# Moving a small transpose, a slot computation and a wait in a two-stage expert kernel, and a longer warm-up

## What is computed

```python
w = cond_weights[itok]                       # 32 x (32 x 32)
xc = einsum('bct,bcd->bdt', x, w)            # 32 x 32 x 256
xt = xc.reshape(T, 256)
probs = softmax(xt @ gate_w)
top_p, top_i = top_k(probs, 2)
for k in range(2):
    e, w = top_i[:, k], top_p[:, k]
    pos = position of the token among those of the same expert
    keep = pos < cap
    buf[e, pos] = xt                         # only where keep
    h = gelu(buf @ w1[e] + b1[e])
    y = h @ w2[e] + b2[e] + gelu(buf @ wd[e]) @ wu[e]
    out += y[e, pos] * keep * w
sh = gelu(xt @ sw1 + sb1) @ sw2 + sb2 + gelu(xt @ swd) @ swu
result = x + out + 0.2 * sh
```

## Time and profile before

| What | us |
|---|---|
| median of three runs | 211.71 |
| the three runs | 211.88, 208.94, 211.71 |
| the profiled execution | 210.92 |
| its span, from first to last instruction | 209.1 |
| outside the span | 1.82 |

### The profile page before, as it was taken

The page is one execution under the profiler, slowest core; times in us unless marked ns, Lnnn a source line. Parts: engine busy times, 40 slices in busy tenths (PEclk is TensorE's granted clock), DMA queues, the critical chain, the costliest instruction groups (busy, mean ns, idle before and its releaser), DMA issues.

```text
span 209.1 us, 3942 instructions
## 1 busy us (share of the span) xinstructions
PE 190.2 (91%) x1390; PEld 182.3 (87%) x1390; DVE 135.0 (65%) x294; ACT 133.9 (64%) x285; POOL 110.3 (53%) x162
## 2 busy tenths in 40 slices
PE   6669999999999499999999999999999999999900
PEld 6667777998789499999999999999999999999900
DVE  4547489744762105695879869869869968967020
ACT  2246799913890107968949949949949859778100
POOL 4401404078773006001794895885876867945662
PEclk9978999999999889999999999999999999999975
DMA  5599971522222895018867867866786787601423
GB/s 164 173 296 336 226 249 48 175 72 85 95 92 72 232 327 196 3 13 287 220 114 231 218 158 210 206 201 194 165 234 199 132 263 223 79 0 9 53 31 39
DMA packets 27897, 33.03 MB, mean 158 GB/s; under 512 B 4554, under 2 KB 24772, under 8 KB 27876
## 3 DMA queue, kind: packets, MB, share of 16 engines
q1 hardware_dynamic: 23748, 27.31, 42.7%
q0 software_dynamic: 3760, 4.89, 14.3%
q10 hardware_dynamic: 368, 0.56, 1.0%
HBM read 23.96 MB, written 8.79 MB: 157 GB/s over the span
## 4 chain that ended last, share of the span: by engine, by line
PE 73%; issue 6%; POOL 6%; DMA 6%; DVE 3%; POOLq 1%; ACT 1%; SPq 1%; DVEq 0%
PE hid_ps L791 10%; PE hid_ps L793 10%; PE hid_ps L792 10%; PE y_ps L791 9%; PE y_ps L793 9%; PE y_ps L792 9%; POOL slot_rows L418 5%; PE turn_ps L935 3%; DMA gate_raw<-in_L_ffn_gate_w 3%; DMA slot_rows<-token_row,slot_i 2%; PE row_ps L951 2%; DMA slot_in<-slot_rows 1%; PE hid_ps L812 1%; POOLq L51 1%; PE turn_ps L812 1%
## 5 line engine op out<-in xcount | busy, mean ns | idle before, releaser
L396 POOL DMA_INDIRECT out_rows<-y_row,slot_tok x24 | 44.8, 1866 | 15.8 <-DVE y_row L735 10.9
L618 DVE TENSOR_TENSOR hid_l<-gelu_f,hid_h 128x320 fp32r<-128x320 f32 (+1 forms) x80 | 41.8, 539 | 12.8 <-ACT hid_h L522 11.1
L791 PE MATMUL hid_ps<-xs_h,w_h 128*128 128x288 f32 x128 | 38.2, 298 | 0.0
L793 PE MATMUL hid_ps<-xs_h,w_l 128*128 128x288 f32 x128 | 37.6, 294 | 0.0
L793 PE MATMUL y_ps<-hid_h,w_l 128*128 128x288 f32 x128 | 37.6, 294 | 0.0
L792 PE MATMUL y_ps<-hid_l,w_h 128*128 128x288 f32 x128 | 37.6, 294 | 0.0
L791 PE MATMUL y_ps<-hid_h,w_h 128*128 128x288 f32 x128 | 37.6, 294 | 0.0
L792 PE MATMUL hid_ps<-xs_l,w_h 128*128 128x288 f32 x128 | 37.6, 294 | 0.0
L521 ACT ACTIVATE gelu_f<-hid_ps,bias_now 128x320 f32<-128x320 f32 x64 | 35.2, 549 | 0.9 <-PE hid_ps L793 0.4
L522 ACT ACTIVATE hid_h<-hid_ps,bias_now 128x320 fp32r<-128x320 f32 x64 | 35.5, 555 | 0.0
L594 DVE TENSOR_TENSOR w_l<-w_raw,w_h 128x512 fp32r<-128x512 f32 x36 | 26.4, 752 | 12.5 <-POOL w_h L364 11.8
(11 more groups left out here) (170 smaller groups left out, 413.9 us busy)
## 6 DMA issues: line engine op xcount, KB each, us to landing
w_raw<-in_L_ffn_w SPq DMA_DIRECT2D x16, 1024.0 KB
slot_rows<-empty_row SPq DMA_DIRECT2D x1, 2600.0 KB, 17.1
slot_in<-slot_rows SPq DMA_DIRECT2D x8, 260.0 KB, 3.7
x_in<-in_x SPq DMA_DIRECT2D x2, 512.0 KB, 4.6
w_raw<-in_L_ffn_sw SPq DMA_DIRECT2D x1, 1024.0 KB
out_rows<-base SPq DMA_DIRECT2D x2, 512.0 KB, 3.8
wu_raw<-in_L_ffn_wu SPq DMA_DIRECT2D x24, 32.0 KB
slot_in<-slot_rows SPq DMA_DIRECT2D x8, 65.0 KB, 3.7
```

Of the source, the lines that this page charges most:

```text
L396: pool.indirect_dma_start(out=out, out_offset=bass.IndirectOffsetOnAxis(ap=slot_tok[par][0:n, s:s + 1].bitcast(U32), axis=0), in_=y_row[0: ...
L618: dve.tensor_tensor(hid_l[:, j - 1, 0:n], gelu_f[:, j % 3, 0:n], hid_h[:, j - 1, 0:n].bitcast(F32), ALU.subtract).then_inc(hid_split, 1)
L791: pe.matmul(out_ap, l_h, r_h, start=start, stop=False)
L793: return pe.matmul(out_ap, l_l, r_h, start=False, stop=stop)
```

## The change

- On VectorE the transpose of the condition and the diagonal copies come ahead of the two chunks of `w1`, not behind them. VectorE makes three of the four copies and ScalarE one (`ACT_DIAG`).
- The warm-up has nine loops in place of five, so 144 matmuls in place of 80.
- `count_before` stands after hidden tile 4 of the first half in place of tile 6, and `place_tokens` after split 5 in place of after split 8.
- `turn_slots(0, 0)` stands after output tile 2 of the second half in place of tile 1, and VectorE's split of the slots after base row 6 in place of 5.

```diff
-WARM_UP = 5
+WARM_UP = 9
+ACT_DIAG = 1
...
-            for g in range(SPT // 2, SPT):
+            for g in range(SPT - ACT_DIAG, SPT):
                 rows = slice(g * C, (g + 1) * C)
                 act.activation(cond_diag[rows, :, rows], diag_v[:, g, :, :], ACT.Copy).then_inc(diag_act, 1)
...
-            for c in range(CHUNKS // 2):
-                w1_chunk(c, 0, 0)
             dve.wait_ge(cond_in, 16)
             dve.transpose(cond_t, cond_dc).then_inc(cond_turned, 1)
             dve.wait_ge(cond_turned, 1)
-            for g in range(SPT // 2):
+            for g in range(SPT - ACT_DIAG):
                 rows = slice(g * C, (g + 1) * C)
                 dve.tensor_copy(cond_diag[rows, :, rows], diag_v[:, g, :, :]).then_inc(diag_dve, 1)
+            for c in range(CHUNKS // 2):
+                w1_chunk(c, 0, 0)
...
                 if j == 2 or j == 3:
                     w2_chunk(CHUNKS // 2 + j - 2, 0, 0)
-            place_tokens()
+                if j == 5:
+                    place_tokens()
...
                 shared_row(t)
-                if t == HTILES + 1:
+                if t == HTILES + 2:
                     slots_lo_part(0)
...
-                pe.wait_ge(diag_dve, SPT // 2)
-                pe.wait_ge(diag_act, SPT - SPT // 2)
+                pe.wait_ge(diag_dve, SPT - ACT_DIAG)
+                pe.wait_ge(diag_act, ACT_DIAG)
...
-                    if h == 0 and j == HT - 3:
+                    if h == 0 and j == HT - 5:
                         count_before()
                 for t in range(HTILES):
                     shared_out(h, t)
-                    if h == 1 and t == 1:
+                    if h == 1 and t == 2:
                         turn_slots(0, 0)
```

## The result

| | median us | runs us | ratio to before, 95% interval |
|---|---|---|---|
| before | 211.05 | 208.94 to 211.88 (4) | |
| changed, the result of record | 215.78 | 215.29 to 216.40 (4) | 1.0265 [1.0202, 1.0329] |
| changed, run again on chip 11 (e9) | 204.21 | 203.81 to 205.36 (6) | 0.9741 [0.9691, 0.9791] |
| changed, on chip 13 (e14) | 204.16 | 203.66 to 204.71 (4) | 0.9718 [0.9668, 0.9769] |
| changed, on chip 9 (e12) | 215.82 | 214.90 to 216.00 (4) | 1.0224 [1.0179, 1.0269] |

The result of record is slower by 2.7% (2.2% by the two medians; the ratio is not their quotient), where 204.9 us and "faster" were forecast. Which chip gave it is not on record. Run again, the same program gave 204.2 twice and 215.8 once. The kernel before lay at 208.5 to 211.9 us in every set of runs.

What follows compares the result with a forecast made beforehand. TensorE was taken to set the end, with holes before the condition matmuls and slot transposes, each followed by half clock. 210.92 - 2.1 (front) + 0.8 (placing) - 4.7 (slot transposes) = 204.9 us, range 203.2 to 207.2.

Steps and rivals of the forecast that it cites:

- the sum: Whole kernel: 210.92 us profiled, less 2.1, plus 0.8, less 4.7, gives 204.9 us, with nothing taken back later.
- part 3: Slots placed after split 5: scatters come 3.1 us earlier, TensorE waits in its first output tile, loss 0.8 us.
- The one slower rival: Warm-up: the clock does not rise during it at all, giving 213.1 us; chance 0.02.
- The range: Forecast limits for the whole kernel, 203.2 to 207.2 us, made of priced cases and scatter of runs.
- Part 1: Front on VectorE: condition transposed first, from about 7.75 to 9.6 us, diagonal ready at 10.8 in place of 12.4 us.
- Part 2: Front: 64 more warm-up matmuls keep the clock up; condition matmuls start 0.4 us earlier and save 1.7 of half clock, 2.1 us.
- the second rival: Warm-up: the clock rises elsewhere in it; earlier gives down to 203.6 us, 2 us later gives 205.9; chance 0.10 for early.
- takes back 1.3 of the 1.6 us: Front: the longer warm-up delays the condition matmuls to 12.1 us, leaving 0.4 us of the earlier start.
- Part 4: Slot transposes after output tile 2: TensorE's 3.05 us wait and some 1.65 us of half clock go, gain 4.7 us.
- The half clock behind a hole: TensorE: soon after each of two holes the granted clock falls to 0.50 for some 3.4 us.

Runs made afterwards that it cites:

- e9: The changed kernel itself, nothing edited, run again on chip 11: 204.21 us, ratio 0.9741.
- e14: The changed kernel itself, nothing edited, run on chip 13: 204.16 us, ratio 0.9718.
- e12: The changed kernel itself, nothing edited, run on chip 9: 215.82 us, ratio 1.0224.
- e8: The changed kernel with the warm-up of before, five loops in place of nine: 204.56 us, ratio 0.9727.
- e5: The changed kernel with GpSimd's wait ahead of its scatters written twice, no work moved: 204.55 us, ratio 0.9748.
- e7: The changed kernel with two diagonal copies on each engine, as before: 203.95 us, ratio 0.9718.
- e13: The kernel before with only the condition's transpose and copies ahead of the weight splits and the slots turned after output tile 2: 204.39 us, ratio 0.9673.
- e18: The kernel before with only the early count and placing, on a sixth chip: 205.68 us, ratio 0.9809.
- e10: The kernel before with only the slots turned after output tile 2 and their low parts a row later: 207.12 us, ratio 0.9785.
- e2: The kernel before with all slot edits (early count and placing, later turning and low parts) and the old front: 206.43 us, ratio 0.9782.
- e1: The changed kernel with the slot edits taken back, so the front edits alone: 207.46 us, ratio 0.9842.
- e3: The changed kernel with only the count and the placing put back: 204.01 us, ratio 0.9687.

## Why the prediction was wrong, and what in it was right

**The step that failed** is in the sum: "Later stages have TensorE full, and all their loads are issued 5 us earlier too, so nothing there takes it back", and in part 3 the sentence that GpSimd is free and its scatters simply come 3.1 us earlier. I priced the earlier scatters by their own end alone and asked only who waits for them. I did not ask what they now run beside: two output tiles whose signals VectorE needs, and ScalarE's wait for the next hidden tile. What the record showed in its place is a wait of 9.5 us and 1.8 us lost at half clock behind it, 11.3 us that the sum did not have. Why the signals come late there stays open, as said above. No rival named it. The one slower rival was a cold warm-up, which did not happen. The range, too, was made of the priced cases and the scatter of before's three runs, 3 us; the changed kernel differs by 11.6 us from one chip to another, more than its whole gain.

The other steps, measured on e14 and e9, where the hole is missing:

- *Part 1.* In e9 the transpose starts at 7.4, the copies at 9.4, and the diagonal is ready at 10.6; in e14 it is 7.9, 9.9 and 11.0 (forecast 7.75, 9.6 and 10.8). Right.
- *Part 2, gain 2.1.* Chains of waits of e9 and of e14:

```profile
4.93 6.64 PE y_ps L801 x116
11.64 1.83 PE hid_ps L814 x16
13.47 1.79 PE turn_ps L814 x16
```

```profile
12.58 1.83 PE hid_ps L814 x16
14.42 1.79 PE turn_ps L814 x16
16.20 0.23 PE hid_ps L830
```

  The scores start at 16.20 (e14), 16.27 (record) and 15.26 (e9) against 17.94: gains of 1.7 and 2.7 around the forecast 2.1. The warm-up ends 0.9 us apart, since its matmuls go to the closer spacing near 5 us in e9 and near 7 us in e14, as the second rival has it. The page TensorE: Matmul & The Clock Gate of the Trainium skill, Part 1, says that the place differs from run to run; these traces agree, with the condition matmuls from 11.64, 12.58 and 12.65 us.
- *But the warm-up does not pay.* e8, with five loops, took 204.56 us, and e5, with nine on the same chip, 204.55. The chain of waits of e8:

```profile
10.14 0.38 DVE cond_diag L627
10.56 3.03 PE hid_ps L814 x16
13.59 2.44 PE turn_ps L814 x16
```

  It runs these matmuls partly at half clock, 5.5 us in place of 3.6, but starts them at 10.56, 2.0 us before e14 does. I had seen that the longer warm-up "takes back 1.3 of the 1.6 us" and then credited it with all of the half clock; the two cancel. The gain at the front is Part 1's. The third copy on VectorE carries none of it under nine loops (e7, 203.95); under five its share is small: e13, with two copies, starts the matmuls at 10.93 and e8 at 10.56.
- *Part 3, loss 0.8.* The second output tile starts at 39.87 before and at 38.58 in e14, 1.3 us earlier for 1.7 won at the front: a loss of 0.4. The splits ran faster behind the placing (0.63 a piece) than the 0.70 assumed. The granted clock stays at 1.00 there.
- *Part 4, gain 4.7.* e14 transposes the slots without a wait:

```profile
69.34 0.65 PE turn_ps L937 x6
72.98 0.13 PE hid_ps L793
```

  The second half's outputs start at 60.18 and expert 0 at 72.98, 12.8 us apart against 17.41: **gain 4.6**. Their loads, issued at 61.03, land some 3 us later, and so 5 us before they are asked for (forecast: over 3). Parts 3 and 4 do each remove the wait alone, as said there: e18 gains 1.9%, e10 2.2%, e2 with both 2.2%, and none of their traces has a wait for the slots.
- *The sum.* e14: 1.7 - 0.4 + 4.6 = 5.9, spans 209.1 and 203.0. Medians against before on the same chips: 6.2 and 6.1 us, forecast 6.0. Where the hole is missing the size of the whole was right, and so were Parts 1 and 4; Part 3's loss was half of the forecast one, and the credit given to the warm-up in Part 2 was wrong. What was missing was a second way for the kernel to go.
- *The half clock behind a hole is not certain*, which the prediction took from one trace. In e1 TensorE waits 2.9 us for the slots, and the granted clock stays at 1.00 from 70 to 74 us; in e18 it waits 3.2 us for the diagonal, and the clock stays at 1.00 from 12 to 16 us; behind e8's 2.8 us it falls to 0.50. The kernel before took 208.5 to 209.1 us in its runs with a mean granted clock of 0.978 or more, and 211.6 to 211.9 in those with 0.957 to 0.959. So up to 3 of the 6 us, an estimate from these two groups, is half clock that the kernel before pays in some runs and not in others.

The kernels to keep are those without the early placing: e3 (0.9687) and e13 (0.9673), not told apart from the changed kernel undisturbed, with the scatters behind the first output tile as before. e13 is two edits and ran undisturbed on the chip on which the changed kernel took 215.8.

## What to carry to other kernels

Moving a burst of transfers earlier is not free because the queue is idle: list what the other engines must tell each other during its new place, and prefer the edit that gains the same wait without moving it. Here turning the slots one tile later did that. And a single start on a single chip is one sample: when a trace shows a wait that ends on nobody ("remote", "unknown queue"), run the same kernel again on another chip before explaining it by the code.

## What the runs showed of the hardware

TensorE's signals came late by 2.5 to 11 us in three traces while its matmuls stand there on time, all during or right behind the scatters of GpSimd. In the run of record five signals in a row were late. The trace has these updates of the semaphores at 47.60, 56.85, 60.41, 60.48 and 60.56 us, the last three 0.08 us apart. The page Perfetto Trace Analysis of the Trainium skill, in its list of a TensorE instruction's stages, says that the shown end of a matmul is computed, and that the signal goes out only when PSUM has acknowledged the writes. That fits a matmul shown at 49 us with a signal at 60; no run here shows which stage was held.

In these traces a scatter takes longer when it begins while a weight split runs on VectorE. The timeline of GpSimd in e14, where VectorE goes on, and in the run of record, where it stands still from 43.2 to 47.6 us:

```profile
43.95 0.97 POOL L419 DMA_INDIRECT slot_rows<-token_row,slot_i  x1 [0.31 <-issue]
45.22 1.42 POOL L419 DMA_INDIRECT slot_rows<-token_row,slot_i  x1 [0.30 <-issue]
```

```profile
45.62 0.98 POOL L419 DMA_INDIRECT slot_rows<-token_row,slot_i  x1 [0.30 <-issue]
46.90 0.97 POOL L419 DMA_INDIRECT slot_rows<-token_row,slot_i  x1 [0.30 <-issue]
48.18 1.31 POOL L419 DMA_INDIRECT slot_rows<-token_row,slot_i  x1 [0.30 <-issue]
```

The long ones (1.42, 1.31) begin 0.1 and 0.2 us after a weight split on VectorE has begun (45.11 and 47.97 us, 0.68 long) and take 0.45 and 0.34 us more than the others: much of what is left of the split. The scatter of 39.09 us in the record, in which the next split only begins (39.49), takes 0.98. Why is not shown.
